# Graph attention on one core: target nodes on partitions, exponentials turned by TensorE, logit rows made one node tile at a time

## What is computed

```python
def gat_layer(x, W, a_src, a_dst, bias, src, dst, heads, out_c, concat):
    h = (x @ W).reshape(n, heads, out_c)
    al_s = jnp.einsum('nhc,hc->nh', h, a_src)
    al_d = jnp.einsum('nhc,hc->nh', h, a_dst)
    e = jax.nn.leaky_relu(al_s[src] + al_d[dst], NEG_SLOPE)
    m = jax.ops.segment_max(e, dst, num_segments=n)
    ex = jnp.exp(e - m[dst])
    z = jax.ops.segment_sum(ex, dst, num_segments=n)
    alpha = ex / (z[dst] + 1e-16)
    msg = h[src] * alpha[:, :, None]
    out = jax.ops.segment_sum(msg, dst, num_segments=n)
```

## Time and profile before

| | us |
|---|---|
| median of three runs (lowest, highest) | 909.38 (904.46, 910.92) |
| the profiled execution | 908.9 |
| its span | 907.1 |
| PE busy in the span | 814.8 (90%) |
| DVE busy | 615.9 (68%) |
| POOL busy | 518.1 (57%) |
| ACT busy | 379.1 (42%) |

### The profile page before, as it was taken

The page is one execution under the profiler, slowest core; times in us unless marked ns, Lnnn a source line. Parts: engine busy times, 40 slices in busy tenths (PEclk is TensorE's granted clock), DMA queues, the critical chain, the costliest instruction groups (busy, mean ns, idle before and its releaser), DMA issues.

```text
span 907.1 us, 10068 instructions
## 1 busy us (share of the span) xinstructions
PE 814.8 (90%) x3992; PEld 634.5 (70%) x3996; DVE 615.9 (68%) x698; ACT 379.1 (42%) x410; POOL 518.1 (57%) x225
## 2 busy tenths in 40 slices
PE   8999998999788999888977699999999997778887
PEld 4569976775555897666554389979987996544564
DVE  8955068999997315899999766557536983633642
ACT  1125266766653335666756333324432431211411
POOL 0347549999995562999999448617652781000000
PEclk9999999999999999999999799999999999759989
DMA  8046426244331751612532275507634635100000
GB/s 358 0 112 223 153 58 176 69 142 139 104 96 44 238 161 55 173 24 74 193 99 83 79 259 177 198 18 276 205 105 172 215 111 208 60 0 1 1 0 35
DMA packets 24262, 110.98 MB, mean 122 GB/s; under 512 B 3604, under 2 KB 5908, under 8 KB 23832
## 3 DMA queue, kind: packets, MB, share of 16 engines
q1 hardware_dynamic: 23096, 104.24, 35.4%
q10 hardware_dynamic: 1120, 6.10, 1.8%
HBM read 100.63 MB, written 0.79 MB: 112 GB/s over the span
## 4 chain that ended last, share of the span: by engine, by line
PE 56%; POOL 28%; DVE 11%; ACT 3%; issue 2%; DMA 0%; DVEq 0%; ACTq 0%
PE ps L955 21%; POOL prod L561 17%; PE ps L903 9%; POOL prod L564 6%; PE ps L940 6%; DVE prod L1705 5%; POOL w_lo L549 4%; PE ps L1333 4%; PE ps L1404 2%; PE ps L1010 2%; PE ps L1031 2%; PE ps L1188 1%; DVE qi_t L1723 1%; PE ps L1310 1%; PE ps L1327 1%
## 5 line engine op out<-in xcount | busy, mean ns | idle before, releaser
L549 POOL TENSOR_TENSOR w_lo<-w_raw,w_hi 128x1536 fp32r<-128x1536 f32 x54 | 201.5, 3743 | 145.0 <-ACT w_hi L615 144.8
L561 POOL TENSOR_TENSOR prod<-prod 128x1024 f32<-128x1024 f32 x94 | 225.2, 2410 | 42.2 <-DVE prod L1705 42.1
L720 ACT ACTIVATE prod<-ps 128x1024 f32<-128x1024 f32 x192 | 187.8, 1024 | 97.6 <-PE ps L1141 74.1
L1705 DVE TENSOR_TENSOR prod<-prod,ps 128x2048 f32<-128x2048 f32 x96 | 218.7, 2278 | 3.2 <-ACT prod L720 2.5
L1141 PE MATMUL ps<-sel_pair,h_and_q 128*128 128x512 f32 x384 | 129.9, 450 | 22.1 <-ACT prod L720 21.8
L903 PE MATMUL ps<-w_raw,h_t 128*128 128x384 f32 x408 | 143.2, 498 | 0.0
L615 ACT ACTIVATE w_hi<-w_raw 128x1536 fp32r<-128x1536 f32 x54 | 80.2, 1488 | 136.6 <-PE ps L955 92.6
L955 PE MATMUL ps<-w_hi,yt_hi 128*128 128x384 f32 x432 | 111.7, 339 | 8.1 <-POOL w_lo L549 8.1
L903 PEld LDWEIGHTS ps<-w_raw,h_t 128*128 128x128 f32 x408 | 79.1, 196 | 46.9 <-issue 3.9
L955 PE MATMUL ps<-w_lo,yt_hi 128*128 128x384 f32 x432 | 110.4, 336 | 0.0
L955 PE MATMUL ps<-w_hi,yt_lo 128*128 128x384 f32 x432 | 110.0, 335 | 0.0
(11 more groups left out here) (194 smaller groups left out, 1017.0 us busy)
## 6 DMA issues: line engine op xcount, KB each, us to landing
w_raw<-weights SPq DMA_DIRECT2D x105, 768.0 KB, 4.4
wa_in<-weights SPq DMA_DIRECT2D x6, 768.0 KB, 5.8
w_gat<-weights SPq DMA_DIRECT2D x6, 768.0 KB, 8.1
w_query<-weights SPq DMA_DIRECT2D x3, 768.0 KB, 11.5
h_and_q<-stage_hi SPq DMA_DIRECT2D x24, 96.0 KB, 2.1
h_and_q<-stage_lo SPq DMA_DIRECT2D x24, 96.0 KB, 2.2
a_vec<-gat_vectors ACTq DMA_DIRECT2D x1, 2048.0 KB, 8.2
q_t<-queries ACTq DMA_DIRECT2D x1, 1536.0 KB, 11.4
```

The costliest lines, as they stand in the source:

```text
L549: pool.tensor_tensor(Wl[:, j, :], raw_slab(U, 0, j), Wh[:, j, :], ALU.subtract).then_inc(w_lo_ready, 1)
L561: pool.tensor_tensor(v[:, :, 0:32], v[:, :, 0:32], v[:, :, 32:64], ALU.add).then_inc(folded_once, 1)
L720: act.activation(slot_view(s)[:, :, 32 * u:32 * u + 32], args.rearrange("p b (n l) -> p (b n) l", l=LH), ACT.Sigmoid).then_inc(sigmoid_rea ...
L1705: TT(slot_view(s), slot_view(s), ps[:, 6, o:o + L].unsqueeze(1).broadcast_to([P, NB, L]), ALU.mult).then_inc(products_ready, 1)
```

## The change

The **target** node goes on partitions for the whole softmax. The pass for the maximum is gone (`masked`, `logit_columns`, `max_rows`, `maxima`, and DVE's instructions with them). `logits` adds into the bank in which `masks` has put the mask, ACT bends the piece, and DVE takes the maximum from the bent piece and negates it (`negated_max`). ACT takes the exponential of each head of 256 columns apart, with that maximum as its per-partition bias. Since `weighted` needs sources on partitions, PE then transposes each 128x128 block of the exponentials (`turn_weights`), and DVE multiplies by the counts as it copies the turned piece out of PSUM (`counted`, now from `ps`). `logit_rows` is done once for each node tile (128 columns), and its split is one ACT and one DVE instruction for each tile, over 40 partitions. The constant `sel_src` (128x1024) and `sel_dst` are made in `attention_counts`. Banks, pieces and all the orders are written anew.

```diff
 BLOCKS = [[[(t, h) for h in range(4)] for t in range(NT)], [[(t, 0) for t in range(NT)]],
-          [[(t, h0 + h) for h in range(4)] for h0 in (0, 4) for t in range(NT)], [[(t, 0) for t in range(NT)]]]
+          [[(t, h0 + h) for h in range(4)] for t in range(NT) for h0 in (0, 4)], [[(t, 0) for t in range(NT)]]]
...
-            def target_rows(g):
-
-                act.wait_ge(g_rows_ready, g + 1)
-                copy(AR[0:GAT[g][0], 1, :], logit_rows_of(g, 1)).then_inc(g_dst_hi, 1)
+            def rows_hi(g, t):
+
+                act.wait_ge(g_rows_ready, 2 * g + t + 1)
+                copy(AR[0:40, t * P:(t + 1) * P], logit_rows_of(t)).then_inc(g_rows_hi, 1)
...
-                act.wait_ge(g_shifted_ready, PBASE[g] + u + 1)
-                _, p = logit_piece(g, u)
-                act.activation(p, p, ACT.Exp).then_inc(g_exp_ready, 1)
+                act.wait_ge(g_max_ready, PBASE[g] + u + 1)
+                for n, (t, h) in enumerate(BLOCKS[g][u]):
+                    block_, col = zb[:, u * 1024 + n * N:u * 1024 + (n + 1) * N], 96 + 8 * t + h
+                    act.activation(block_, block_, ACT.Exp, bias=small[:, col:col + 1]).then_inc(g_exp_ready, 1)
...
+            rows_hi(0, 0)
             keep_h(0, 0)
-            target_rows(0)
+            rows_hi(0, 1)
             leaky(0, 0)
             leaky(0, 1)
-            keep_h(0, 1)
             exponential(0, 0)
             exponential(0, 1)
+            keep_h(0, 1)
...
                 n = IN_CHUNKS[g]
                 for k in range(n):
-                    ins = pe.matmul(ps[0:40, 7, 0:N], Wa[:, WB[g] + k, :], HT[:, k, :], start=(k == 0), stop=(k == n - 1))
+                    ins = pe.matmul(logit_rows_of(t), Wa[:, WB[g] + k, :], HT[:, k, t * P:(t + 1) * P],
+                                    start=(k == 0), stop=(k == n - 1))
                 ins.then_inc(g_rows_ready, 1)
...
+            def turn_weights(g, u):
+
+                p, b0 = BLOCKS[g][u], TURN_BANKS[g][u]
+                for n in range(len(p)):
+                    pe.wait_ge(g_exp_ready, EBASE[g] + sum(len(q) for q in BLOCKS[g][:u]) + n + 1)
+                    for s in range(NT):
+                        o = u * 1024 + n * N + s * P
+                        ins = pe.transpose(turned_piece(g, u).rearrange("p b n -> p (b n)")[:, (s * len(p) + n) * P:
+                                                                                           (s * len(p) + n + 1) * P],
+                                           zb[:, o:o + P], ident[:])
+                ins.then_inc(g_exp_turned, 1)
...
-                dve.tensor_scalar(AR[:], ident[0:64, 0:1].unsqueeze(2).broadcast_to([64, 2, N]), 0.0, None, ALU.mult)
+                dve.tensor_scalar(AR[:], ident[:, 0:1].broadcast_to([P, N]), 0.0, None, ALU.mult)
+                TT(sel_src[:], ident[:, 0:SELK].unsqueeze(2).broadcast_to([P, SELK, P]),
+                   ident[:, 64:64 + SELK].unsqueeze(2).broadcast_to([P, SELK, P]), ALU.add)
+                TT(sel_dst[:], ident[:, 32:32 + SELK], ident[:, 96:96 + SELK], ALU.add)
...
+            def negated_max(g, u):
+
+                p = BLOCKS[g][u]
+                t, h = p[0]
+                mx = small[:, 96 + 8 * t + h:96 + 8 * t + h + len(p)] if len(BLOCKS[g]) > 1 else small[:, 96:112:8]
+                dve.wait_ge(g_leaky_ready, PBASE[g] + u + 1)
+                dve.tensor_reduce(mx, zb[:, u * 1024:u * 1024 + len(p) * N].rearrange("p (h n) -> p h n", n=N),
+                                  AX.X, ALU.max).then_inc(g_max_found, 1)
+                dve.wait_ge(g_max_found, PBASE[g] + u + 1)
+                dve.tensor_scalar(mx, mx, -1.0, None, ALU.mult).then_inc(g_max_ready, 1)
```

More of the change, by code:

```diff
@@ L867, in _ @@
             relu_norm(3, 1, norm_h_ready)
-            target_rows(2)
-            keep_h(2, 0)
+            rows_hi(2, 0)
+            rows_hi(2, 1)
             leaky(2, 0)
@@ L874, in _ @@
             exponential(2, 1)
+            keep_h(2, 0)
             leaky(2, 3)
@@ L1375, in logits @@
                 ins.then_inc(g_logits_ready, 1)
-            def max_rows(g):
-                hn = GAT[g][0]
-                pe.wait_ge(g_max_ready, g + 1)
-                for t in range(NT):
-                    ins = pe.transpose(max_rows_of(g)[:, t, :], small[:, 96 + hn * t:96 + hn * (t + 1)], ident[:])
-                ins.then_inc(g_max_transposed, 1)
-            def maxima(g, h0):
-                n = min(GAT[g][0], 4)
-                for h in range(n):
-                    ins = pe.matmul(block_of(max_bank(g), h), selb[0:64, h0 + h, :], MR[:], start=True, stop=True)
-                ins.then_inc(g_maxima_ready, 1)
+            def turn_weights(g, u):
[8 more added lines that the diff above has]
+                ins.then_inc(g_exp_turned, 1)
@@ L1480, in _ @@
[L1480 to L1489 removed]
+            logits(2, 0)
+            logits(2, 1)
+            projection(2, 0, 3, 5)
+            pe.wait_ge(g_leaky_ready, PBASE[2] + 1)
             masks(2, 2)
[L1491 removed]
+            logits(2, 2)
@@ L1513, in _ @@
+            turn_weights(2, 1)
+            projection(2, 1, 3, 6)
+            pe.wait_ge(g_leaky_ready, PBASE[2] + 4)
+            turn_weights(2, 2)
+            pe.wait_ge(g_weights_ready, PBASE[2] + 1)
+            turn_weights(2, 3)
             pe.wait_ge(g_h_copied, 6)
-            pe.wait_ge(g_weights_ready, PBASE[2] + 2)
             for d in range(NT):
-                weighted(2, d, 0, 4, 2 * d, False)
-            pe.wait_ge(g_weights_ready, PBASE[2] + 4)
-            for d in range(NT):
-                weighted(2, d, 4, 8, 2 * d + 1, True)
@@ L1991, in _ @@
             norm_shift(3, 1)
+            ones_column(2)
+            rows_lo(2, 0)
             second_half(3, 6, 6, False)
-            gat_weights(2)
-            heads_out(2, 0, 0, 2)
-            heads_out(2, 1, 2, 2)
+            rows_lo(2, 1)
+            negated_max(2, 0)
+            negated_max(2, 1)
+            negated_max(2, 2)
+            counted(2, 0)
+            negated_max(2, 3)
+            for u in range(1, 4):
+                counted(2, u)
+            for d in range(NT):
+                heads_out(2, d, SUM_BANKS[2][d], 2)
             for t in range(NT):
@@ L2004, in _ @@
             ch.step(ins)
-            gat_weights(3)
+            ones_column(3)
+            for t in range(NT):
+                rows_lo(3, t)
+            negated_max(3, 0)
+            counted(3, 0)
             for d in range(NT):
-                one_head_out(3, d, two_banks(6 * d), ps[:, 6 * d + 1, FH:FH + 1], halves(X[:, d, :]),
+                bank = SUM_BANKS[3][d]
+                one_head_out(3, d, two_banks(bank), ps[:, bank + 1, FH:FH + 1], halves(X[:, d, :]),
                              halves(X[:, d, :])).then_inc(result_ready, 1)
```

336 lines of the change are left out of this document (127 added, 209 removed).

## The result

| | before | changed |
|---|---|---|
| median of the runs, us | 908.16 (904.46 to 910.92, 4 runs) | 885.25 (885.03 to 886.23, 4 runs) |
| the profiled execution's span | 907.1 | 883.2 |
| PE busy in the span | 814.8 | 802.7 |

The changed kernel takes 0.9753 of the time of before, 95% interval 0.9729 to 0.9778: 22.9 us less. The direction was right, the size was not: 14.8 us were forecast.

What follows compares the result with a forecast made beforehand. PE bounds attentions 2 and 3; chains of small dependent steps and the low clock bound 0 and 1. Gains 3.8 + 4.2 + 6.1 + 0.7 = 14.8 us gave 894.1, or 894.5 beside the median; range 887 to 902.

Steps and rivals of the forecast that it cites:

- The half rows: Logit rows for one node tile, 12 records of 128 columns on PE: taken as 1.35 us, at most 2.77.
- the rival of dear transposes: Attention 2: each transpose waits for its exponential, 0.24 not 0.118 us; 56 cost 6.8 us more, 901.3; chance 0.19.
- the wait at the split: Attention 3: second half rows wait for a split behind DVE's two additions into x, 0.4 us lost.
- neither collision: Ahead of the attentions: DVE's shift could make one POOL collision, 1.5 us, more or fewer; counted as 0.
- I take `weighted` at the low clock: Attention 0: 16 x 0.22 = 3.5 us for each target tile; the attention's gain 3.8 us.
- Attention 1, all at the low clock: Attention 1: 18.2 us becomes 14.0 with PE at the lower clock throughout, gain 4.2 us.
- the clock holds in attention 0: Attention 0's sparse transposes keep the clock; weighted, attention 1 and the perceptron get shorter: 884.5 us; chance 0.11.
- T to W2: From attention 2's first transposes (T) to its weighted (W2): weighted starts 3.9 us earlier.
- attention 1's steps: Attention 1: from tile 1's output through rows, logits, exponentials, weighted and division, summed to 14.0 us.
- attention 3's terms: Attention 3: 1.1 us removed, 0.5 added, 0.4 lost at the split, h_t 0.35 sooner; gain 0.7 us.
- W2 to W3: Attention 2's weighted (W2) to attention 3's (W3): 1.7 us from high clock, 0.5 earlier division, 0.7 attention 3.
- Of the 0.8 us lost at the low clock at the start I count nothing won: Attention 3's start: 0.8 us lost at the low clock before, taken to stay lost.

Runs made afterwards that it cites:

- e9: Changed kernel without attention 2's 32 transposes, counted reading the exponentials in place: 882.20 us, ratio to before 0.9719.
- e4: Kernel before with 38 filler transposes in PE's idle time ahead of attention 0's weighted: 900.27 us, ratio to before 0.9921.
- e7: Changed kernel with 13 filler matmuls, 8 among attention 0's transposes and 5 behind them: 882.91 us, ratio to before 0.9719.
- e12: Kernel before once more, unchanged, with a second profile: 906.37 us, ratio to before 0.9989.
- e1: Kernel before with its 64-row selector matmuls padded with zero rows to 128: 902.76 us, ratio to before 0.9957.
- e2: Changed kernel with logits reading only 64 rows instead of 128: 887.12 us, ratio to before 0.9787.
- e5: Changed kernel, attention 0 reordered: ACT splits logit rows ahead of keep_h, DVE folds attention 1's vectors behind counted: 882.39 us, ratio to before 0.9718.
- e6: Changed kernel, splits ahead of keep_h, folding behind counted, exponential table loaded early, attention 3's additions between its splits: 881.09 us, ratio to before 0.9695.
- e8: Changed kernel without attention 0's 16 transposes, counted reading the exponentials in place: 887.06 us, ratio to before 0.9765.
- e10: Changed kernel, attention 0 reordered, table early, attention 3's additions moved, plus 8 filler matmuls among attention 0's transposes: 882.42 us, ratio to before 0.9718.
- e3: Kernel before with 20 filler matmuls in PE's idle time ahead of attention 0's weighted: 899.61 us, ratio to before 0.9932.
- e11: Changed kernel once more, unchanged: 886.23 us, ratio to before 0.9758.

## Why the prediction was right and wrong

**Right.** The work of every stage was laid out correctly. In attention 0 the steps that set the start of `weighted` came within about 0.1 us (second logits, exposed table, folding, start at 780.72). The half rows cost 1.44 to 1.5 us. The transposes cost 0.109 to 0.111 us each (0.118 forecast), so the rival of dear transposes (0.24 each, a price that no row gave) is excluded, in attention 2 directly by e9. There `weighted` had no gap ahead of it and ran at the high clock. Attention 3 did get the wait at the split, 0.69 us (0.4 forecast). `attention_counts` was hidden, and POOL's last three took 14.98 or 14.99 us in all fourteen profiles, so neither collision came.

**Wrong: the clock up to T.** The failed steps are "I take `weighted` at the low clock", "Attention 1, all at the low clock", and the perceptron, for which the sum has no gain. Together they gave 8.0 us up to T, and it was 13.6. The low clock lasted 10.2 us and not 30 or more. Of the 5.6 us missing, `weighted` of attention 0 is 1.2 (5.82, not 7.06), the perceptron 1.9, and attention 1 2.4, of which 1.8 are its `weighted` (1.98, not 3.78). How much of the 13.6 is work? With the clock up nearly all the way T lies at 78.45 for before (e4) and at 71.14 for the changed kernel (e7). e4 still lost some 1.05 us in attention 1's `weighted` (3.03, not 1.98), and e7's fillers delayed attention 0's `weighted` by 0.25. So about 6.5 us are less work on the path, and about 7 are the clock. That split is an estimate from one profile each of two kernels with fillers, the shortest execution of either. A second estimate agrees: over all executions the changed kernel has 24 us less low clock in the whole program (50 and 74 on the mean), which at the 0.27 us each of e12's section is 6.5 us.

The rival "the clock holds in attention 0" named 884.5, near the result, but it did not happen as it was written: the clock fell, 1.3 us into `weighted`. The near match is luck: it comes from 3.45 us elsewhere that no case had.

**Wrong: T to W2.** 3.9 us forecast, 6.3 measured, with 3.4 us of low clock at its start in both kernels. The missing term is the switching between 64 and 128 rows, seven excursions that came to 2.1 of the 2.4 us (e1 against e4, and e2). The other 0.3 is in the sum: its own terms (4.2 removed, 3.8 added, 3.85 of gaps) give 4.2 and not 3.9. Two more stages don't add up: attention 1's steps give 13.7 us and not 14.0, attention 3's terms 0.55 and not 0.7. The price of switching was in the trace of before: two projections at the high clock, of the same 4 records, stood 1.49 and 1.38 us apart from what followed, by whether 64-row matmuls stood on both sides. I had priced removed matmuls at their own spacing and kept the neighbours' price.

**Sized too small: W2 to W3.** 1.7 and 0.5 for attention 2 and 0.7 for attention 3, 2.9 in all; 3.95 measured. `weighted` gave 1.73. "Of the 0.8 us lost at the low clock at the start I count nothing won": in the changed kernel (both profiles) that was won, in e5, e6 and e8 to e10 it was not, and their W2 to W3 is 0.8 to 0.9 us longer. The rest is again rows of 64: e1's stretch is 0.57 longer than before's, but its `weighted` lost 1.4 more to the clock, so without that it is 0.8 shorter. Against this stands the wait at the split, 0.3 more than forecast.

**Open.** What sets where the clock falls and rises is not settled. That filling PE's idle time with matmuls or transposes keeps it up is shown (e3, e4, e7), and that 16 sparse transposes put off its fall (e8). That it was up again from about 792 in the changed kernel is only observed (in e2, e8 and e11 at about the same place, in e9 some 2 us earlier). That before has 41 us or more of low clock and the changed kernel 14 is seen in two profiles each, and the difference in all executions; that the removed idle times are the cause is argued, not shown.

## What to carry to other kernels

Where PE has idle stretches, take the time at the lower clock as a quantity of its own with a spread, and don't carry one execution's course of it into the forecast; a second profile of the kernel before would have shown that. Look for matmuls with fewer rows among full ones: padding them with zero rows to 128 showed no cost here and saved 0.3 to 0.4 us for each excursion. When an instruction is taken from one place in a queue, look at what stands behind the new place: the folding cost attention 0 its time ahead of `counted`, and most of it again behind it.

## What was not expected of the hardware

- Transposes kept TensorE's clock up as matmuls did: 38 in 4.37 us, `weighted` 3.76 us in both (e3, e4); and 16 sparse ones put off its fall (5.82 against 7.06 us in e8).
- Going from 128-row to 64-row matmuls and back costs PE 0.3 to 0.4 us at the high clock (2.58 and 2.20 us for the same piece, e1; 1.17 us for three, e2; 2.1 for seven, e1 against e4).
- The same program showed 34.1 and 23.9 us of low clock over the same stretch in two executions (before and e12), and their times agree all the same, 0.9989 (0.9969 to 1.0009).
